# A residual added by an identity matmul and copied out by ScalarE, in place of a fused sum on VectorE

## The reference

```
x2  = x  + nearest(gn(x))        # each pixel replaced by its nearest of 256 words, if near enough
out = x2 + mamba_conv(gn(x2))
mamba_conv(v): layer norm over channels -> 4 chunks of 64 channels
    per chunk: in_proj, causal conv of 4 taps, silu, x_proj -> dt, B, C
        state scan h[t] = exp(dt*A) * h[t-1] + dt*u*B   (128 channels x 16 states, 1024 steps)
        y = sum(h*C) + u*D, times silu(z), out_proj, plus skip
    layer norm over 256 channels, then y = y @ proj_w.T + proj_b
```

## Time and profile before

| | |
|---|---|
| median of 3 runs | 4431.4 us (4430.06 to 4437.95) |
| the profiled execution | 4433.55 us, its span 4431.7 us |
| busy share of the span | VectorE 90%, TensorE 85%, GpSimd 77%, ScalarE 63% |
| granted clock of TensorE, mean | 0.932 of full speed |
| DMA queue of SyncE | 65.7% of the 16 DMA engines' time |

### The profile page before, as it was taken

The page is one execution under the profiler, slowest core; times in us unless marked ns, Lnnn a source line. Parts: engine busy times, 40 slices in busy tenths (PEclk is TensorE's granted clock), DMA queues, the critical chain, the costliest instruction groups (busy, mean ns, idle before and its releaser), DMA issues. The chain is left out here.

```text
span 4431.7 us, 44302 instructions
## 1 busy us (share of the span) xinstructions
PE 3779.5 (85%) x13840; PEld 1269.6 (29%) x13840; DVE 4003.7 (90%) x3073; ACT 2810.5 (63%) x3528; POOL 3427.9 (77%) x2086
## 2 busy tenths in 40 slices
PE   3688988988888898888989888888988988888896
PEld 2222323223232232323223232232323323232221
DVE  2589899998989999899999989999899998989996
ACT  2566666666666666666666666666666666666653
POOL 2487787787878878888778788787788778788775
PEclk8898998999989999998999989999998999989997
DMA  1657576675757758576675767757576675767763
GB/s 39 154 143 193 149 189 177 174 192 152 190 157 188 201 135 202 148 192 180 167 197 143 200 159 186 201 140 202 140 196 183 164 197 144 198 162 186 193 166 109
DMA packets 217723, 751.74 MB, mean 170 GB/s; under 512 B 27400, under 2 KB 28816, under 8 KB 213392
## 3 DMA queue, kind: packets, MB, share of 16 engines
q1 hardware_dynamic: 217488, 748.91, 65.7%
HBM read 639.75 MB, written 75.50 MB: 161 GB/s over the span
## 5 line engine op out<-in xcount | busy, mean ns | idle before, releaser
L592 POOL TENSOR_TENSOR state<-state,c_all 128x1024 f32<-128x1024 f32 x1024 | 2400.1, 2362 | 252.0 <-DVE state L953 229.5
L953 DVE TENSOR_TENSOR_SCAN state<-dtb,ub 128x1024 f32<-128x1024 f32 x1024 | 2341.0, 2286 | 42.7 <-ACT dtb L795 6.1
L1182 PE MATMUL ub<-u,spr 64*128 64x512 f32 x4096 | 1271.5, 683 | 352.1 <-DVE state L953 349.6
L795 ACT ACTIVATE dtb<-dtb,a_neg 128x1024 f32<-128x1024 f32 x1024 | 1159.7, 1141 | 389.4 <-DMA dtb<-dt_scratch 379.8
L944 DVE TENSOR_TENSOR ub<-ub,b_all 128x1024 f32<-128x1024 f32 x1024 | 1243.1, 1214 | 105.0 <-PE ub L1182 98.8
L1182 PEld LDWEIGHTS ub<-u,spr 64*128 64x128 f32 x4096 | 347.8, 196 | 1160.2 <-DVE state L953 679.6
L1198 PE MATMUL yp<-state,gat 128*32 128x512 f32 x4096 | 583.0, 643 | 6.1 <-POOL state L592 6.1
L1047 PE MATMUL mb<-xs,wtap 128*128 128x512 f32 x512 | 261.4, 657 | 20.1 <-DMA xs<-xn 10.6
L668 ACT ACTIVATE dt<-mb 128x512 f32<-128x512 f32 x128 | 75.8, 592 | 241.7 <-PE mb L1078 241.7
L643 ACT ACTIVATE e_x<-mb,ncb 128x512 f32<-128x512 f32 x128 | 88.0, 687 | 219.1 <-PE mb L1047 219.1
L1061 PE MATMUL mb<-xc,wdt 128*128 128x512 f32 x256 | 153.1, 683 | 78.3 <-ACT ym L715 55.4
(11 more groups left out here) (143 smaller groups left out, 4821.6 us busy)
## 6 DMA issues: line engine op xcount, KB each, us to landing
dtb<-dt_scratch SPq DMA_DIRECT2D x1024, 512.0 KB, 4.8
xs<-xn SPq DMA_DIRECT2D x128, 256.0 KB, 5.3
b_all<-bc_scratch SPq DMA_DIRECT2D x64, 512.0 KB, 6.4
c_all<-bc_scratch SPq DMA_DIRECT2D x64, 512.0 KB, 7.9
xt<-in_x SPq DMA_DIRECT2D x16, 1024.0 KB, 6.6
x_scratch<-xt SPq DMA_DIRECT2D x16, 1024.0 KB, 7.0
dt_scratch<-dt SPq DMA_DIRECT2D x64, 256.0 KB, 3.4
dt_scratch<-dt SPq DMA_DIRECT2D x128, 128.0 KB, 3.6
```

Source lines behind the costliest of these rows:

```text
L592: pool.tensor_tensor(v, v, c_all[:, c % 2, :], ALU.mult).then_inc(gated, 1)
L795: act.activation(dtb[:, k, :], dtb[:, k, :], ACT.Exp, scale=a_neg[:, GROUP[g]:GROUP[g] + 1]).then_inc(decayed, 1)
L953: dve.tensor_tensor_scan(state[:, g % STATES, :], dtb[:, k, :], ub[:, g % 2, :], 0.0, ALU.mult, ALU.add).then_inc(scanned, 1)
L1182: last = pe.matmul(ub[:, g % 2, h * HALF:(h + 1) * HALF], spr[lo:lo + TURN, GROUP[g] % 8, :], u[lo:lo + TURN, c % 2, h * HALF:(h + 1) * HA ...
```

## The change

`c_out` moves from VectorE's list to ScalarE's, in the same slots, and becomes an activation that reads the bank, adds the bias and writes `res`. The sum with x2 moves to TensorE: each `c_proj` begins with a matmul of the fp32 identity `idf` (128 x 128) with the piece of `res`, into the same bank. The wait for x2 moves with it.

```diff
-             (1, 17): ["post_take0", "post_take1"], (1, 24): ["a_sum10"], ...
+             (1, 17): ["post_take0", "post_take1"], (1, 29): ["c_out00", "c_out01"], (1, 31): ["c_out10", "c_out11"], (1, 24): ["a_sum10"], ...
...
-             (1, 28): ["a_gm1"], (1, 29): ["c_out00", "c_out01"], (1, 31): ["c_out10", "c_out11"],
+             (1, 28): ["a_gm1"], 
...
+                elif name.startswith("c_out"):
+                    q, mm = int(name[-2]), int(name[-1])
+                    bank, use = banks(kind, b, (name.replace("out", "proj"), 0))
+                    act.wait_ge(m_full[bank], use)
+                    act.activation(res[:, mm, q * HALF:(q + 1) * HALF], mb[:, bank, :], ACT.Identity,
+                                   bias=pb2[:, mm:mm + 1]).then_inc(m_free[bank], 1)
...
-                elif name.startswith("c_out"):
-                    h, mm = int(name[-2]), int(name[-1])
-                    cut = slice(h * HALF, (h + 1) * HALF)
-                    dve.wait_ge(s_x2ld, 16 * b)
-                    bank, use = banks(kind, b, (name.replace("out", "proj"), 0))
-                    dve.wait_ge(m_full[bank], use)
-                    dve.scalar_tensor_tensor(out=res[:, mm, cut], in0=mb[:, bank, :], scalar=pb2[:, mm:mm + 1],
-                                             in1=res[:, mm, cut], op0=ALU.add, op1=ALU.add).then_inc(m_free[bank], 1)
...
                     pe.wait_ge(cl_n, 2 * (b - 1) + h + 1)
+                    pe.wait_ge(s_x2ld, 16 * b)
                     bank = enter(kind, b, (name, 0))
+                    pe.matmul(mb[:, bank, :], idf[:], res[:, mm, h * HALF:(h + 1) * HALF], start=True, stop=False)
                     for j in range(NJ):
                         last = pe.matmul(mb[:, bank, :], wp[:, h, j, mm * P:(mm + 1) * P],
-                                         cd[:, j, h * HALF:(h + 1) * HALF], start=(j == 0), stop=(j == NJ - 1))
+                                         cd[:, j, h * HALF:(h + 1) * HALF], start=False, stop=(j == NJ - 1))
```

More of the change, by code:

```diff
@@ L832, in _ @@
             turn(LAST, NB - 1)
-            for name in ("post_take0", "post_take1", "c_sq0", "c_sq1", "c_msq0", "c_rs0", "c_msq1", "c_rs1"):
+            for name in ("post_take0", "post_take1", "c_sq0", "c_sq1", "c_msq0", "c_rs0", "c_msq1", "c_rs1",
+                         "c_out00", "c_out01", "c_out10", "c_out11"):
                 do(name, "tail", NB, 0)
@@ L1020, in _ @@
             turn(LAST, NB - 1)
-            for name in ("post_gate", "c_var0", "c_ctr0", "c_var1", "c_ctr1", "c_out00", "c_out01", "c_out10", "c_out11"):
+            for name in ("post_gate", "c_var0", "c_ctr0", "c_var1", "c_ctr1"):
                 do(name, "tail", NB, 0)
```

## The result

| | before | changed |
|---|---|---|
| median, first comparison | 4432.3 us (4 runs) | 4507.9 us (4 runs, 4501.4 to 4522.5) |
| ratio, 95% interval | | 1.0173 (1.0147 to 1.0200) |
| the profiled execution, its span | 4433.55, 4431.7 us | 4501.43, 4499.6 us |
| median, compared once more | 4438.9 us (9 runs) | 4520.3 us (5 runs) |
| ratio, 95% interval | | 1.0189 (1.0175 to 1.0203) |

The change makes the kernel 1.7 to 1.9% slower. The forecast was 4496 us, 1.5% slower; the profiled execution has 67.9 us more span where my sum was 65.0, the medians have 76 and 81 more. Of the runs of the changed kernel the profiled one is the fastest.

A forecast was written before the change was run, and what follows sets the result against it. TensorE, not the busier VectorE, was taken to set the pace at the projections. Loop 55.0, clock 3.4, last turn 3.2 and tail 3.4 sum to 65.0 us, on 4431.4 giving 4496 us, 8-in-10 range 4466 to 4516.

The forecast's parts named there:

- the forecast's own case: The prediction's main case, slower at 4496 us: chance 0.70, with its own range of 4484 to 4508 us.
- the wider range: The prediction's 8-in-10 range for the time: 4466 to 4516 us.
- the clock: TensorE at 1.2 GHz in a_mean0: two more images with the fall, at 1.7 us each, 3.4 us.
- the last turn: Last turn, without an affine: only TensorE's part stays, the multiply of (2, 0) is 3.2 us late.
- the tail: End of the kernel: four more matmuls, 3.5 us, less 0.07 for ScalarE's shorter step: 3.4 us.
- What bounds the stretch: Around the projections TensorE sets the pace, not VectorE; VectorE's sums gone alone would give back some 0.1 us per image.
- The identity matmuls: Ahead of the projections: 0.90 us each, nothing hides them; VectorE 3.5 us late at the multiply of (2, 0).
- The copies: c_out on ScalarE: first pair costs nothing; second, behind the affine, 1.15 us, holding banks and the next decay.
- The affine: On ScalarE, it waits until the last projection is full and is 3.35 us late.
- The stretch in sum: Multiply of (1, 14) to that of (2, 2): 10 images at 3.9 us, 4 at 4.0, 55.0 in all.
- The rival in which more is lost: Clock falls in all images and at new places, or costlier held banks and decay: 4510 to 4520 us, chance 0.12.

The follow-up runs named there:

- e3: Kernel before with VectorE's sum cut to one column of 512, all waits kept: 4431.1 us, ratio 1.0000.
- e2: Kernel before with the identity matmuls on TensorE; VectorE still reads the banks and adds the bias only: 4469.4 us, ratio 1.0081.
- e1: Changed kernel without its identity matmuls, so x2 isn't added; ScalarE's copies stay: 4429.7 us, ratio 0.9996.
- e9: Changed kernel with the affine's squares written to a free tile, so the affine no longer waits for the projections: 4459.4 us, ratio 1.0051.
- e4: Kernel before with two filling fp32 matmuls in TensorE's idle ahead of a_mean0 in the loop: 4406.8 us, ratio 0.9942.
- e5: Changed kernel with c_out10 and c_out11 ahead of the affine on ScalarE instead of behind it: 4514.6 us, ratio to before 1.0181.
- e8: e5 with the two filling matmuls of e4 ahead of a_mean0: 4477.6 us, ratio 1.0094.

## Why the prediction was right, and where it was short

The measured 4507.9 us is 12 above the forecast, at the very end of the 4484 to 4508 that I gave the forecast's own case. The second comparison's 4520.3 is above the wider range, and its distance from before, 81.4 us, just within it. The mechanism at the projections is right; mis-sized is the clock. That the profiled execution has 67.9 where my sum has 65.0 is partly luck: the 14 stretches lost 2.6 less than the sum, the last turn and the tail 2.1 less, the first turn is 2.4 shorter where the sum has nothing, and chunk 0 is some 10 longer where it has nothing either.

**What bounds the stretch (right).** TensorE, not VectorE. e3 shows that VectorE's sums are worth nothing, e2 that TensorE's matmuls are paid nearly in full (3.2 us of time per stretch for 3.4 of matmuls).

**The identity matmuls (right, a little dear).** 0.86 us each by the timeline, 0.90 in the sum. Alone they cost 3.2 per stretch (e2), where the sum had 3.35. The multiply of (2, 0) comes 12.50 after the scan of (1, 14), 3.4 later than before (9.09); forecast 3.5. By the Trainium skill's gap for one matmul (TensorE: Matmul & The Clock Gate, Back-to-back issue gap) the time would have been near 4451, by my estimate. The trace disagrees for fp32, with 0.86 us for one matmul where that gives 0.216.

**The copies (right in sum, wrong alone).** I put the first pair at nothing because ScalarE idles; in the changed kernel that holds. e1 shows that this leans on the longer projections: without them bank 0 is given back 0.61 late and the affine waits for TensorE. The second pair holds `a_mean0` back as forecast (released by L768).

**The affine (right).** It is 3.2 late, forecast 3.35, and TensorE releases it. e9 takes its wait away, and of the stretch 1.2 us go, with all slow `a_mean0`. The other 2.7 would be lost without it.

**The stretch in sum (right).** 23.65 beside 19.7, 3.95 where I had 4.0. Over 14 images 351.1 - 295.3 = 55.8 us, where the sum had 55.0 and 3.4 for the clock. That is 2.6 less than forecast. A slow stretch costs 3.8 more than a slow one of before (25.19 beside 21.38), where I had 3.9. `a_mean0` was slow in 13 images, and in 14 in the second trace, where I had counted 12. By the stretches with a low clock it is 11 before and 13 now, so there are the two more that I had counted.

**Last turn (right) and tail (short, and hidden by luck).** VectorE idles 2.55 and 2.92 in the last turn, whose stretch is 3.05 longer, forecast 3.2. From the last turn's start to the end it is 285.6 where it was 281.1: 4.5 us, 6.6 forecast. That looks close, but the tail's projections take 12.24 instead of 7.11 us, 5.1 more where I had 3.5: the first of the four groups runs at a granted clock of 0.61, its three matmuls in 4.35 us instead of 2.57. And the work just ahead of it, matmuls of the means for the most part, came out 3.0 shorter, at a granted clock of 0.85 where before had 0.68. In the second trace of the changed kernel that clock is 0.67, and the last turn and the tail cost 8.35 more than before. VectorE in the last turn, then TensorE and ScalarE in the tail:

```profile
4334.20 1.23 DVE L943 TENSOR_TENSOR ub<-ub,b_all 128x1024 f32<-128x1024 f32 x1 [2.55 <-PE ub L1183]
...
4340.68 1.23 DVE L943 TENSOR_TENSOR ub<-ub,b_all 128x1024 f32<-128x1024 f32 x1 [2.92 <-PE ub L1183]
```

```profile
4482.25 1.69 PE L1152 MATMUL mb<-xn,idf 128*128 128x512 f32 x2 [2.07 <-DVE cd L932]
4483.73 3.03 PE L1154 MATMUL mb<-cd,wp 128*128 128x512 f32 x4
```

```profile
4494.52 0.69 ACT L768 ACTIVATE xn<-mb,pb 128x512 f32<-128x512 f32 x1 [1.89 <-PE mb L1154]
```

**The term that was too small: the clock.** I had 3.4 us for it, all at `a_mean0`. The medians are 76 and 81 us up, and the sum of what was forecast elsewhere is 62. In the profiled execution 67.9 - 55.8 - 4.5 = 7.6 us are left. In the 14 images the first eight units take 10.2 more (438.8 to 449.0 us), where no instruction was changed, the first turn takes 2.4 less, and every other part of a turn is within 1.2 of before. In these eight units an image takes either about 31 or about 33.5 us, and the longer ones have the lower clock. Before, 2 of 14 were of the long kind, with the change 6. Two images of the kernel before (columns: stretch, its length, busy us of TensorE, its weight loads, VectorE, ScalarE and GpSimd, granted clock, DMA share, GB/s):

```profile
952.23:983.51 31.28, 23.08 (x85) 6.49 (x81) 28.54 (x19) 20.09 (x29) 26.32 (x21) 0.94 0.68 177
1219.24:1252.70 33.46, 27.42 (x81) 7.62 (x81) 28.69 (x19) 21.27 (x29) 27.52 (x21) 0.76 0.69 180
```

and two of the changed one:

```profile
954.21:987.79 33.58, 26.59 (x81) 7.36 (x82) 28.72 (x20) 21.03 (x29) 27.31 (x21) 0.80 0.67 177
1776.62:1807.74 31.12, 22.98 (x85) 6.49 (x81) 28.54 (x19) 20.71 (x29) 26.17 (x21) 0.94 0.70 182
```

VectorE's busy time is nearly the same in all four; the 2.2 us between the two of before are waits for a slower TensorE. Most of them stand ahead of the ninth unit:

```profile
983.51 1.23 DVE L944 TENSOR_TENSOR ub<-ub,b_all 128x1024 f32<-128x1024 f32 x1 [2.51 <-PE ub L1182]
1252.70 1.23 DVE L944 TENSOR_TENSOR ub<-ub,b_all 128x1024 f32<-128x1024 f32 x1 [4.08 <-PE ub L1182]
```

The other traces show the same in chunk 0 (sums over 14 images, with the granted clock, and the images where the second half of `a_norm` takes 3.57 us instead of 1.95):

| kernel | units 0 to 7 | clock | units 8 to 15 | clock | slow `a_norm` |
|---|---|---|---|---|---|
| before | 438.8 us | 0.885 | 524.2 us | 0.917 | 7 |
| changed | 449.0 | 0.851 | 523.6 | 0.916 | 7 |
| changed, again | 450.0 | 0.857 | 527.6 | 0.909 | 8 |
| e1 | 431.2 | 0.872 | 540.1 | 0.867 | 14 |
| e2 | 440.5 | 0.881 | 513.7 | 0.944 | 5 |
| e4 | 434.7 | 0.879 | 515.3 | 0.938 | 6 |
| e5 | 461.4 | 0.809 | 531.3 | 0.894 | 10 |
| e8 | 441.3 | 0.866 | 535.6 | 0.881 | 12 |

These kernels have the same instructions there. In units 8 to 15 the time goes with the clock. In units 0 to 7 it does so less strictly: e1 is the shortest at 0.872, so it also counts which matmuls the low clock meets. Across executions the mean clock goes with the time as well: the nine timed runs of the changed kernel go from a span of 4499.6 at 0.932 to 4524.5 at 0.919. The timed runs of before have 0.930 to 0.936.

So in the traced executions the loss at unchanged places lies in waits for TensorE at a lower clock. For the medians, whose losses are 8 and 14 us above that of the profiled execution and which were not traced, it is argued from the mean clock alone. Why the changed kernel falls into the long kind more often is open. No experiment took the falls in chunk 0 alone away from the changed kernel: e4, e8 and e1 removed them at `a_mean0`, and in e8 and e1 the second half of `a_norm` was slow more often. The rival in which more is lost ("falls in all images and at new places") is in part what happened: in the second trace `a_mean0` is slow in all 14 images, and in both more images are long in the first eight units.

## What to carry to other kernels

Before you move work off the engine with the highest busy share, look at the place where the work stands: with the waits around it 45.8 us of VectorE were worth nothing, and four matmuls of 0.86 us on the engine that set the pace there cost 2.7 to 3.2 of the 4 us per image. Look also at what reuses a tile or a bank behind the longer work; the affine's wait, made only by where it put its squares, cost 1.2 us per image and the clock at `a_mean0`, and taking it away gave 49 of the 76 us back (e9). Where TensorE idles a little in each turn, a few filling matmuls in the idle can be the cheapest gain of all, but measure each: the first of mine brought 0.6%, the one added to it nothing.

## What I had not expected of the hardware

- The fall of TensorE's clock doesn't follow from the idle ahead of an instruction alone. `a_mean0` was slow in 10 of 14 images after an idle of 1.9 us (before), in none of 14 after 2.36 (e1), in 13 of 14 after 2.36 (changed), in 4 of 14 after 1.70 (e2).
- So a change of a few tenths of a us per turn can move the time by more than its own size: e1 costs 1.08 us per stretch and the time stayed (0.9996). In its trace 17 us of slow stretches were gone, and the low clock stood at `a_norm` in all 14 images instead of 7.
- In these traces an fp32 matmul of 128 x 512 is two records and takes 0.86 us from start to start at 2.4 GHz, with the identity as with other weights.
